# Token experts of a four-layer gated cross-attention model: GpSimd's row loads two groups further ahead of its result stores

## Reference

```
def _combine_weights(logits):
    vals, idx = jax.lax.top_k(logits, K)          # K = 2 of E = 8
    ...
def _ffn(h, w1, b1, w2, b2):
    return jax.nn.gelu(h @ w1 + b1, approximate=False) @ w2 + b2
def _token_moe(h, gw, gb, w1, b1, w2, b2):
    cw = _combine_weights(h @ gw + gb)
    out = jnp.zeros_like(h)
    for e in range(E):
        out = out + _ffn(h, w1[e], b1[e], w2[e], b2[e]) * cw[..., e:e + 1]
```

## Time and profile before

| | |
|---|---|
| median of 3 runs | 1676.03 us (1674.0 to 1676.31) |
| profiled execution, its own time | 1660.98 us |
| its span | 1659.6 us |
| TensorE matmul busy | 1539.6 us, 93% of the span |
| VectorE / ScalarE / GpSimd busy | 747.2 / 680.7 / 241.7 us |
| token expert stage, first row load to last result store | 803.8 to 970.3 us |
| mean granted TensorE clock | 0.97 of full speed |

### The profile page before, as it was taken

One profiled execution on the slowest core, in us unless ns is written; L12 is line 12 of the kernel. 1 busy time (PEld: TensorE's weight loads), 2 busy tenths in 40 slices (PEclk: granted clock), 3 DMA queues, 4 the chain that ended last, 5 costly groups with the idle time before them and its releaser, 6 DMA issues.

```text
span 1659.6 us, 32141 instructions
## 1 busy us (share of the span) xinstructions
PE 1539.6 (93%) x12101; PEld 1272.0 (77%) x12101; DVE 747.2 (45%) x2634; ACT 680.7 (41%) x2151; POOL 241.7 (15%) x379
## 2 busy tenths in 40 slices
PE   7999999799989999998699978999999999999986
PEld 5787887688977777775588866878987777777865
DVE  3535565411036666864011157771124443444466
ACT  2615433322117676754233326643334443344452
POOL 2022210000001121212311133156000000000000
PEclk9999999899999999998799999889999999999999
DMA  9500011359210100401789910337930001000000
GB/s 335 204 1 1 1 42 38 115 204 292 49 54 1 55 2 2 182 2 47 238 301 310 309 36 24 103 102 239 300 109 1 1 1 38 1 1 2 1 1 23
DMA packets 103253, 156.38 MB, mean 94 GB/s; under 512 B 12231, under 2 KB 80959, under 8 KB 102535
## 3 DMA queue, kind: packets, MB, share of 16 engines
q1 hardware_dynamic: 97515, 143.53, 26.2%
q0 software_dynamic: 3552, 9.18, 1.6%
q10 hardware_dynamic: 2048, 1.84, 0.3%
HBM read 147.31 MB, written 11.67 MB: 96 GB/s over the span
## 4 chain that ended last, share of the span: by engine, by line
PE 70%; ACT 7%; DMA 5%; DVE 5%; issue 3%; POOL 2%; POOLq 0%; ACTq 0%; DVEq 0%
PE psum L581 43%; PE psum L678 6%; PE psum L662 5%; PE psum L702 5%; PE psum L968 5%; ACT arena L889 4%; DMA arena<-token_rows 3%; DMA expert_out<-arena 1%; PE psum L537 1%; POOL token_rows L1272 1%; PE psum L955 1%; ACT arena L903 1%; PE psum L710 1%; PE psum L547 1%; DVE arena L801 1%
## 5 line engine op out<-in xcount | busy, mean ns | idle before, releaser
L889 ACT ACTIVATE arena<-arena,rowmin 112x375 f32<-112x375 f32 (+1 forms) x584 | 292.6, 507 | 180.4 <-DVE rowmin L801 180.3
L581 PE MATMUL psum<-arena,region 128*128 128x112 f32 (+2 forms) x1920 | 325.6, 327 | 5.2 <-DMA arena<-in_ctxT 2.6
L581 PEld LDWEIGHTS psum<-arena,region 128*128 128x128 f32 x1920 | 261.9, 197 | 66.1 <-issue 5.6
L581 PE MATMUL psum<-region,arena 128*125 128x128 f32 (+4 forms) x1632 | 230.5, 291 | 9.8 <-DVE arena L790 3.7
L581 PEld LDWEIGHTS psum<-region,arena 128*125 128x125 f32 (+2 forms) x1632 | 195.5, 183 | 44.1 <-issue 18.7
L678 PEld LDWEIGHTS psum<-identity,arena 112*125 112x125 f32 (+1 forms) x1240 | 141.8, 177 | 57.9 <-ACT arena L903 17.2
L678 PE MATMUL psum<-identity,arena 112*125 112x112 f32 (+1 forms) x1240 | 165.8, 278 | 15.8 <-ACT arena L903 5.0
L581 PE MATMUL psum<-arena 128*128 128x128 f32 (+4 forms) x896 | 141.4, 315 | 0.0
L662 PE MATMUL psum<-arena 32*112 32x375 f32 (+3 forms) x912 | 133.6, 477 | 0.5 <-DVE arena L779 0.4
L581 PEld LDWEIGHTS psum<-arena 128*128 128x128 f32 (+2 forms) x896 | 125.9, 192 | 10.5 <-issue 0.3
L949 POOL COPY arena<-rinv 112x128 f32<-112x128 f32 x136 | 34.0, 293 | 581.7 <-DVE rinv L824 558.9
(11 more groups left out here) (304 smaller groups left out, 1891.9 us busy)
## 6 DMA issues: line engine op xcount, KB each, us to landing
stream<-in_moe_w SPq DMA_DIRECT2D x36, 1024.0 KB, 7.3
arena<-in_moe_w SPq DMA_DIRECT2D x36, 1024.0 KB, 7.3
arena<-in_ctxT SPq DMA_DIRECT2D x32, 375.0 KB, 4.2
stream<-in_e_wg SPq DMA_DIRECT2D x8, 512.0 KB, 4.6
stream<-in_e_wu SPq DMA_DIRECT2D x8, 512.0 KB, 5.7
stream<-in_e_wd SPq DMA_DIRECT2D x8, 512.0 KB, 6.6
region<-in_e_wg SPq DMA_DIRECT2D x8, 512.0 KB, 7.6
region<-in_e_wu SPq DMA_DIRECT2D x8, 512.0 KB, 8.4
```

Of the source, the lines that this page charges most:

```text
L581: last = pe.matmul(dst, l, r, start=(i == 0), stop=(i == n - 1))
L889: last = act.activation(e, e, ACT.Exp, bias=rowmin[:, j, n:n + 1], scale=-1.0, accum_out=rowsum[:, j, h:h + 1])
```

## The change

GpSimd's row loads run two groups further ahead. Two more loads, of groups 2 and 3, are issued before the loop, each after T(0) or T(1). In the loop, step r waits for T(r+2) and loads group r+4; then it waits for the copied result of group r and stores it. In the old order step r waited for T(r), loaded r+2 and stored r-1, with two stores in the last step. The buffers are the same two: a load of group g+2 still needs T(g) to be done. Two more groups are loaded past the end, so `token_rows` grows from 26 to 28 groups of 128 rows, and the zeroing near the program's start with it (256 KB more). The wait after the loop counts the two more loads. TensorE's, VectorE's, ScalarE's and SyncE's lists keep their order.

```
-        tok_rows = nc.dram_tensor("token_rows", ((MAX_TURNS * TOK_SLOTS + 2) * P, C), F32, kind="Internal").ap()
+        tok_rows = nc.dram_tensor("token_rows", ((MAX_TURNS * TOK_SLOTS + 4) * P, C), F32, kind="Internal").ap()
...
             load(tok_rows.rearrange("(c p) f -> c p f", p=P),
-                 A["zeros"].unsqueeze(0).broadcast_to([MAX_TURNS * TOK_SLOTS + 2, P, C]), s_zero)
+                 A["zeros"].unsqueeze(0).broadcast_to([MAX_TURNS * TOK_SLOTS + 4, P, C]), s_zero)
...
             for r in range(2):
                 chunk_rows(0, r)
+            p = p_m[0]
+            for r in range(2):
+                wait_first(g, *p["tok_turned"].at(0, r))
+                chunk_rows(0, r + 2)
             with g.Fori(0, turns) as it:
-                p = p_m[0]
                 for r in range(TOK_SLOTS):
-                    wait_first(g, *p["tok_turned"].at(it, r))
-                    chunk_rows(it, r + 2)
-                    for n in ([r - 1] if r else []) + ([r] if r == TOK_SLOTS - 1 else []):
-                        wait_first(g, *p["tok_y_kept"].at(it, n))
-                        g.dma_start(tok_outs[bass.ds((it * TOK_SLOTS + n) * P, P), :], tok_y[n])\
-                            .then_inc(s_yst[n % 2], 16)
+                    wait_first(g, *p["tok_turned"].at(it, r + 2))
+                    chunk_rows(it, r + 4)
+                    wait_first(g, *p["tok_y_kept"].at(it, r))
+                    g.dma_start(tok_outs[bass.ds((it * TOK_SLOTS + r) * P, P), :], tok_y[r])\
+                        .then_inc(s_yst[r % 2], 16)
             for s in range(2):
-                wait_first(g, s_xr[s], turns * (8 * TOK_SLOTS) + 16)
+                wait_first(g, s_xr[s], turns * (8 * TOK_SLOTS) + 32)
```

## The result

| | before | changed |
|---|---|---|
| median, first comparison | 1676.03 us (5 runs, 1671.76 to 1678.96) | 1664.46 us (5 runs, 1659.93 to 1668.06) |
| ratio to before, 95% interval | | 0.9936 (0.9920 to 0.9952) |
| ratio, second and third comparison | | 0.9941 (0.9918 to 0.9963), 0.9937 (0.9915 to 0.9958) |
| profiled execution's span | 1659.6 us | 1666.6 us |
| first row load to last result store | 803.8 to 969.73: 165.9 us | 811.1 to 966.94: 155.8 us |

The change gains 11.6 us by the medians of the first comparison; the interval of its ratio is 8 to 13.4 us. The ratios leave out three executions that took 2545 to 3706 us, two of the kernel before and one of the larger array alone. Oddly, the changed kernel's profiled execution is 7 us longer than that of before. The five executions of either kernel spread over 7 to 8 us, so single spans can't be compared to a few us.

A forecast was written before the change was run, and what follows sets the result against it. TensorE, busy 93% of the span, was taken as the bound; eight row-load waits, 8.0 us idle plus 0.22 us each, give 9.8 us, the added work 0: 1676.03 - 9.8 = 1666.2 us, range 1661.7 to 1671.5.

The forecast's parts named there:

- The eight waits: TensorE's row-load waits before T(5) and T(6), turns 1 to 4: 8.0 us idle plus about 0.22 each, 9.8 us gone.
- What makes the loads late: Row loads stand behind result stores in GpSimd's list and land in 6.0 us median, 7.2 at most, under weight loads.
- Are the new loads on time?: Load of group g+2 leaves after T(g); shortest way, T(3) to T(5), is 10.9 us, with 2.5 us to spare.
- GpSimd's loads start within 0.8 us of each T: Sign of being right in the changed profile: each GpSimd row load starts at most 0.8 us after its T.
- What is late next?: Weights must keep up with 29.0 us turns: 321 GB/s needed, 381 seen; H(5) of slot 1 has least time.
- The added work: Two more row loads and 256 KB more zeros: taken as 0, the zeros between 0 and 0.8 us.
- The total: Median of the whole kernel: 1676.03 - 9.8 = 1666.2 us.
- The spread allowed for the clock: Stretches at 1.2 GHz may fall differently after the stage: 3 us allowed both ways.
- longer waits in the unprofiled runs: Waits in the stage may be longer without the profiler: 1.5 us taken off the range's lower end.
- The DMA bound: Rival, 6%: the stage can't hold more than 310 GB/s, turns take 30.0 us, total about 1671.5 us.
- the late weights: Rival, 4%: expert weights land late at H(5), four turns lose 6.4 us, total about 1682 us.
- The rival that the gain isn't there: Rival, 4%: row loads take 2.3 us, TensorE waited for something the change does not move; time stays at 1676.

The follow-up runs named there:

- second and third comparison: The changed kernel with no further edit, measured again against the kernel before: ratios 0.9941 (0.9918 to 0.9963) and 0.9937 (0.9915 to 0.9958).
- three profiles of the old order: The kernel before, profiled twice, and that kernel with only the row array and its zeroing grown to 28 groups: stages 165.9, 164.6 and 166.1 us.
- the extra traffic: Changed kernel plus a 1 MB copy within the chip's memory behind each group's weights from the second turn on: stage 174.5 us, 18.7 more than the change.

## Why the prediction came out right

*The eight waits.* Right in size and in place: none is left, O(2) to O(3) and O(3) to O take 3.67 and 10.82 us, forecast 3.68 and 10.8. From the first O on, the profile of before, on which the 9.8 us were reckoned, is 148.6 us and the changed ones 138.9: 9.7 us. That each wait costs about 0.2 us beyond its idle time holds in all three profiles of the old order, whose eight waits are 8.0, 6.9 and 7.6 us of idle time and cost 9.7, 8.5 and 9.3; by the named idle time alone the sum would have been 8.0. That the mean of the whole stage, 9.9, comes so near 9.8 is in part luck: the eight waits of the three profiles cost 9.2 us in the mean, and 0.7 us is the first turn's.

*What makes the loads late.* Place and landing together, as argued: either one removed takes all eight waits. What the prediction did not have is that the two waits are coupled, 2.2 us of 5.4 coming back when only the first goes. In the whole change this doesn't matter, because both loads are ahead.

*Are the new loads on time?* Yes. "GpSimd's loads start within 0.8 us of each T" was wrong for one of four: the load behind T(5) starts 1.8 us after it, because it still stands behind the store of O(2). It goes out at 877.11, and its T comes at 893.01: 15.9 us.

*What is late next?* Nothing: the turn takes 28.98 us, forecast 29.0; 326 GB/s, forecast 321. The bound of the DMA engines, put at 381 GB/s from a stretch of before, showed itself at 394 with the extra traffic, which is of another kind in part, and at H(5) as named.

*The added work.* The two further row loads hold nothing up, since the gather still starts behind the last store's landing; the zeros can't be told from nothing (1.0008, 0.9980 to 1.0036), within a bound far wider than the 0.8 us in question.

*The total.* Forecast 1666.2, measured 1664.46. The 1.7 us between them is below what the comparison can tell; the other two comparisons gave ratios of 0.9941 and 0.9937, 9.9 and 10.6 us. The spread allowed for the clock, 3 us both ways, was too small for single executions, which move by 7 us in the part ahead of the stage alone. It was enough for two of the three medians; the third, 1660.82 beside 1674.68 for before, is 4.1 us below what a gain of 9.8 would give. No run shows the 1.5 us that the range allowed for longer waits in the unprofiled runs; the further profiles of the old order had shorter ones.

*The rivals.* The DMA bound and the late weights are ruled out by the stretch with TensorE busy throughout, and the run with extra traffic shows what they would have looked like. The rival that the gain isn't there fell with the eight waits.

## What to carry to other kernels

When an engine issues both loads and stores from one list, a load that stands behind a store waits for the result as well as for its buffer; put it directly behind the instruction that frees the buffer. Size its lead by the landing time beside the other traffic of the stage, not by the time of the transfer alone, and look at every place where the consumer's order bunches its uses. Where a program's time scatters by several us, compare the stage in several profiles: here that told 10 us to within 1. Its part behind whatever scatters, here from the first O on, came out alike to 0.01 us in three profiles of the changed kernel.

## What I had not expected of the hardware

The same instructions ahead of the stage took 804 to 811 us in executions of one and the same kernel, and the profiled spans of one kernel went from 1656.4 to 1666.6 us, with the mean granted clock at 0.967 and 0.962. An estimate from these numbers: 109 and 127 us at 1.2 GHz, 17 us more, and a busy TensorE loses half of that, 8.7 of the 10.2 us. Stretches at 1.2 GHz fall differently in each execution, enough to hide a gain of 10 us between two single profiles. And taking one wait away brought two 2 MB loads closer together (3.7 us in place of 4.8); the row loads behind them took 6.3 us in place of 5.6, and 2.2 us came back in four turns.
